# Rope and transpose of each batch's ten tiles moved to slots of their own in a fused attention and mixture kernel

## The reference

```
q = rms_norm(layernorm(x)) * q_norm_w       # 16 heads of 32
k = rms_norm(ctx) * k_norm_w ; v = ctx      # 4 key/value heads, 4 query heads on each
q, k = q*cos + rotate_half(q)*sin, the same for k          # rope
x = x + softmax(causal(q k^T / sqrt(32))) v @ w_out.T
xt = layernorm(x)
probs = softmax(xt @ w_router); top 4 of 128, normalised
basis_k = silu(xt @ w_gate_k) * (xt @ w_up_k)               # k = 0..7, 256 wide
mixed = sum over the top 4 and k of mix * basis_k ; x = x + mixed @ w_down + shared(xt)
```

## Time and profile before

| | |
|---|---|
| runs | 840.81, 843.52, 844.84 us; median 843.52 us |
| the profiled execution | 844.43 us, its span 842.7 us |
| PE | busy 780.9 us (93%) |
| DVE | busy 656.7 us (78%) |
| ACT | busy 578.7 us (69%) |
| POOL | busy 523.7 us (62%) |
| mean granted TensorE clock | 0.974 |
| transfers | 127.02 MB, mean 151 GB/s |

### The profile page before, as it was taken

The page is one execution under the profiler, slowest core; times in us unless marked ns, Lnnn a source line. Parts: engine busy times, 40 slices in busy tenths (PEclk is TensorE's granted clock), DMA queues, the critical chain, the costliest instruction groups (busy, mean ns, idle before and its releaser), DMA issues. The chain is left out here.

```text
span 842.7 us, 15205 instructions
## 1 busy us (share of the span) xinstructions
PE 780.9 (93%) x4180; PEld 617.7 (73%) x4180; DVE 656.7 (78%) x1635; ACT 578.7 (69%) x1413; POOL 523.7 (62%) x685
## 2 busy tenths in 40 slices
PE   2768899899999999989999999989999999999998
PEld 2645567677777778667778788768777887788876
DVE  7657798679888778778888888767878786688774
ACT  3867887577777667677688676658776775654542
POOL 4546457895488556896378745896566624661561
PEclk9967799999999999999999999989999999999999
DMA  8322135445445545643454445435444535454550
GB/s 289 110 67 80 31 131 169 137 142 176 152 157 169 155 154 201 197 142 126 148 204 167 138 136 181 161 126 169 149 165 142 176 116 163 164 187 128 207 190 26
DMA packets 57051, 127.02 MB, mean 151 GB/s; under 512 B 10920, under 2 KB 28040, under 8 KB 56968
## 3 DMA queue, kind: packets, MB, share of 16 engines
q1 hardware_dynamic: 56968, 126.04, 45.1%
HBM read 107.55 MB, written 4.46 MB: 133 GB/s over the span
## 5 line engine op out<-in xcount | busy, mean ns | idle before, releaser
L1606 PE MATMUL u<-w_h,t_h 128*128 128x512 f32 x640 | 259.6, 406 | 9.4 <-POOL w_l L888 7.1
L1606 PE MATMUL u<-w_l,t_h 128*128 128x512 f32 x640 | 251.7, 393 | 0.0
L1606 PE MATMUL u<-w_h,t_l 128*128 128x512 f32 x640 | 251.6, 393 | 0.0
L1259 DVE TENSOR_TENSOR w_l<-w_raw,w_h 128x512 fp32r<-128x512 f32 x288 | 244.8, 877 | 0.0
L930 ACT ACTIVATE w_h<-w_raw 128x512 fp32r<-128x512 f32 x384 | 218.9, 620 | 11.3 <-DMA w_raw<-in_w_units 10.5
L888 POOL TENSOR_TENSOR w_l<-w_raw,w_h 128x512 fp32r<-128x512 f32 x96 | 138.2, 1439 | 102.1 <-ACT w_h L930 101.7
L964 ACT ACTIVATE scores<-scores,mx 128x384 f32<-128x384 f32 (+1 forms) x224 | 128.3, 573 | 76.9 <-DVE mx L1202 75.4
L1202 DVE CUSTOM_DVE_ANT_0 scores<-s,mask_qk 128x384 f32<-128x384 f32 (+1 forms) x224 | 112.3, 503 | 49.0 <-PE s L1482 48.3
L1606 PEld LDWEIGHTS u<-w_h,t_h 128*128 128x128 f32 x640 | 121.4, 190 | 37.9 <-POOL w_l L888 9.9
L896 POOL TENSOR_TENSOR macc<-macc,gb 128x256 f32<-128x256 f32 x112 | 105.0, 939 | 64.6 <-DVE gb L1362 64.4
L1606 PEld LDWEIGHTS u<-w_h,t_l 128*128 128x128 f32 x640 | 120.9, 189 | 27.2
(11 more groups left out here) (150 smaller groups left out, 1208.1 us busy)
## 6 DMA issues: line engine op xcount, KB each, us to landing
w_raw<-in_w_units SPq DMA_DIRECT2D x160, 512.0 KB, 4.2
w_raw<-in_w_out_t SPq DMA_DIRECT2D x16, 512.0 KB, 4.9
w_raw<-in_shared_w_down SPq DMA_DIRECT2D x16, 512.0 KB, 4.5
q_st<-turned_h SPq DMA_DIRECT2D x232, 32.0 KB, 1.9
out<-x SPq DMA_DIRECT2D x16, 256.0 KB, 2.2
q_st<-turned_l SPq DMA_DIRECT2D x116, 32.0 KB, 1.9
x<-in_x SPq DMA_DIRECT2D x3, 1024.0 KB, 9.5
k_st<-turned_h SPq DMA_DIRECT2D x48, 32.0 KB, 2.3
```

Source lines behind the costliest of these rows:

```text
L1259: e.tensor_tensor(w_l[:, i % WR, k, :], w_raw[:, i % WR, k, :], f32(w_h[:, i % WR, k, :]), ALU.subtract).then_inc(s_wl, 1)
L1606: last = e.matmul(u_bank[n % 2][:], t[:, k, cols], ww[:, i % WR, k, :], start=(k == 0 and m == 0), stop=(k == KC - 1 and m == 2))
```

## The change

All ten tiles of a batch get slots of their own, written as offsets from the batch's first slot, one table for batch 1 and one for batches 2 and 3. In absolute slots, from before to after:

| tile of batch 1 | rope | turn |
|---|---|---|
| 10 (keys) | 31 → 33 | 34 → 36 |
| 11 | 37 → 36 | 40 |
| 12 | 43 → 39 | 46 → 43 |
| 13 | 49 → 42 | 52 → 46 |
| 14 | 53 → 45 | 56 → 50 |
| 15 (keys) | 54 → 48 | 57 → 56 |
| 16 | 57 → 51 | 60 |
| 17 | 61 → 59 | 64 |
| 18 | 65 → 64 | 68 → 69 |
| 19 | 73 → 69 | 76 → 74 |

In batch 2 (batch 3 is 48 slots later, but for its last tile, 170 → 165 and 173 → 171): tile 20 79 → 74, 82 → 79; 21 stays at 81 and 84; 22 89 → 85, 92 → 89; 23 97 → 88, 100 → 92; 24 101 → 92, 104 → 97; 25 102 → 95, 105 → 104; 26 105 → 99, 108; 27 109 → 107, 112; 28 113 → 112, 116 → 117; 29 121 → 117, 124 → 123. In batch 0 only the rope of tile 9 moves, 30 → 27. The key squares and scales, query scale and moments of the second halves come 2 to 10 slots earlier, the keys' stacking 2 slots later (first halves) or 1 earlier (second halves). The stacking of queries keeps its slot, except that it follows a later turn (tiles 18, 28, 38: one slot later). No instruction is added or removed.

```diff
-FIRST_TILES = dict(rope=(-34, -32, -20, -12, -7, 6, 9, 16, 23, 30), turn=(-17, -13, -8, -1, 6, 12, 15, 21, 27, 34), stack=(7, 16, 22, 28, 35))
+FIRST_TILES = dict(rope=(-34, -32, -20, -12, -7, 6, 9, 16, 23, 27), turn=(-17, -13, -8, -1, 6, 12, 15, 21, 27, 34), stack=(7, 16, 22, 28, 35))
+SECOND_TILES = dict(rope=(-19, -16, -13, -10, -7, -4, -1, 7, 12, 17), turn=(-16, -12, -9, -6, -2, 4, 8, 12, 17, 22))
+LATER_TILES = dict(rope=(-26, -19, -15, -12, -8, -5, -1, 7, 12, 17), turn=(-21, -16, -11, -8, -3, 4, 8, 12, 17, 23))
...
-QUERY = dict(rope=-3, turn=0, stack=1)
-KEYS = dict(rope=(-21, 2), turn=(-18, 5))
-
-PREP = dict(key_squares=(-39, 4, -29, -8), key_scale=(-36, 5, -26, -1), query_scale=(-35, 9, -23, 4), key_stack=(1, 13, -16, 8))
+
+PREP = dict(key_squares=(-39, 4, -29, -10), key_scale=(-36, 5, -26, -7), query_scale=(-35, 9, -23, -6), key_stack=(1, 13, -14, 7))
...
-MOMENTS = (-39, -38, 4, 7, -32, -27, -6, -1)
+MOMENTS = (-39, -38, 4, 7, -32, -27, -13, -9)
...
-            hb, i = n // NB, n % NB
-            if hb < H:
-                return FIRST_TILES[name][n]
-            if i == 0:
-                return batch_slot(hb // H) + KEYS[name][hb % H]
-            return span_slot(hb * KV + i - 3) + QUERY[name]
+            b, i = n // (H * NB), n % (H * NB)
+            return batch_slot(b) + (FIRST_TILES, SECOND_TILES, LATER_TILES)[min(b, 2)][name][i]
...
-                if s == (FIRST_TILES["stack"][u - U0] if u < H * KV else span_slot(u - 2) + QUERY["stack"]):
+                if s == (FIRST_TILES["stack"][u - U0] if u < H * KV
+                         else max(span_slot(u - 2), tile_slot(query_tile(u), "turn")) + 1):
```

## The result

The changed kernel takes 852.42 us (median of 4 runs, 850.83 to 854.38) against 843.55 us for the kernel before beside it: ratio 1.0111, 95% interval 1.0078 to 1.0144. It is 1.1% slower, where 831.5 us, 1.4% faster, was forecast, and it lies above the range given (826 to 841). The profiled execution took 852.83 us with a span of 851.1 us; before, the span was 842.7 us.

What follows compares the result with a forecast made beforehand. TensorE, busy 780.9 of 842.7 us, was taken as the bound, with GpSimd late at batch borders; 15.2 - 1.5 - 1.0 = 12.7 us off 844.43 gave 831.7, stated as 831.5 us, range 826 to 841.

Steps and rivals of the forecast that it cites:

- SyncE's order: First halves' keys stacked behind maxima and queries instead of before; TensorE waits for none of them, so no cost.
- The ring of turned buffers: `turned_high` must wait for the stacking of the tile two before; cost nothing, up to 1 us at the high end.
- VectorE's added work: Batch 1: two moments and a low part earlier, at slots 39 and 43; with tile 10's later turn, 0 to 3, taken 1.0 us.
- the banks: Moving TensorE's transposes among the three rotating banks, bounded by 0.5 us either way.
- The ports' rule: VectorE and GpSimd lock each other out for whole instructions; ropes against eight `w_l` would cost 6 us, not 0.7.
- Borders, 15.2 gross: TensorE's waits at three batch borders go, 10.4 us, and the clock falls behind them, 4.8 us.
- the floor: The chain projection, VectorE's residual and moments, `norm_scale`, `w_l` keeps 0 to 1.1 us at three borders; taken 0.5 each.
- Tiles 21 and 31, 1.40 us, stay: TensorE's waits of 1.40 us before these tiles remain, as their slots are unchanged.
- The rival "slower, 851 us": New GpSimd backlog in batch 1's slots 42 to 53, 6.3 us a place, three places deciding; chance 0.08.
- the time until slot 44 longer by over 2 us: Sign of being wrong: the start, 110.05 us until slot 44 before, lengthens by over 2 us.
- a batch of 48 slots: Sign of being right: 48 slots take about 190 us in place of 194.
- `turned_high` waiting for transfers: Sign of being wrong: `turned_high` waits for stacking transfers.

Runs made afterwards that it cites:

- the earlier load: Kernel with early keys and VectorE's work back, plus SyncE's shared w_down load started one slot earlier: 831.6 us, ratio 0.9866.
- the three mends: Changed kernel with first halves' keys stacked early again, second halves' key squares two slots later, shared w_down load one slot earlier: 830.54 us, ratio 0.9859.

## Why the prediction was wrong, by its own steps

**SyncE's order, priced at nothing: the step that failed.** The prediction saw that the keys of a first half are stacked behind the queries and said that TensorE waits for none of these transfers. True, and beside the point: what stands behind them in the queue is a weight load for which ScalarE waits, with VectorE's `d_l` and TensorE behind it. So the time that SyncE's issues take, which the sum had at nothing, is what was mis-priced. Twelve issues of 0.63 us make it start 6.7 us later. Measured: 13.5 us in two places, 14 us by the experiment that moves the keys back (852.42 to 838.47), and 13.3 us by the one that moves them late in the kernel before. Of the 7.1 us of slots 88 to 90, 3.84 are the wait and 10 x (1 - 0.72) = 2.8 the clock of that window; of the 6.5 us of slots 136 to 138, 4.31 and 10 x (1 - 0.83) = 1.7.

**The ring of turned buffers, "cost nothing, up to 1 us".** Right for the tiles that it is about: after 44 us no `turned_h` waits for a transfer in the changed kernel. The prediction worked it out for tiles 33 and 35, slot 152; the tighter place is tile 22, whose turn comes three slots after the keys of tile 20 are stacked. There the slack is some 4 us by the estimate above, and the 4.97 us wait needs the load in front of the keys.

**VectorE's added work and the banks, 0 to 3 us, taken 1.0, and 0.5 us either way for the banks.** Measured: 4.9 us at slot 46 in the profile, 3.2 to 3.7 us in time, from the squares of a key tile, which the prediction did not name (it priced moments and a low part, which proved free). 1.75 us of it are the wait; the rest goes, by the inference above, with the clock behind it, which the prediction had at 1.00 from slot 46 on. The bank order makes it a wait of 2.50 us, and half a microsecond was no bound for that: what a bank costs is the lateness of its reader. The ports' rule, set at 6 us for the ropes against the adds, did not come in that size: all 288 `w_l` of VectorE are busy for 248.1 us, where it was 244.8. But in one place a pair took 2.35 us in place of 1.28, and that was where TensorE waited.

**Borders, 15.2 gross, 1.5 for the floor.** Right. 4.8 + 4.0 + 6.2 = 15.0 us came back, where 13.7 were forecast. The three waits for `w_l` left 0.70, 0.74 and 0.69 us, within the 0 to 1.1 given, and the clock in both windows is 1.00. The stretches behind the borders took 1.3 to 2.0 us each, together 4.7, a term that the sum lacked: that is SyncE's queue too, as the earlier load shows.

**Tiles 21 and 31, 1.40 us, stay.** Right: 1.40 and 1.33 us.

**The sum.** Without the late keys and the squares the changed kernel takes 835.1 us, 7.8 below the kernel before beside it, where 12.0 were forecast; with the load early too it takes 830.5. That this is near 831.5 is in part luck: the earlier load is no part of the change, and it also takes from a wait that the kernel before had (0.73 us for `d_l` at 200.36 us). The gain of the borders was there; what was missed is what the move displaced. The rival "slower, 851 us" had the size, but not the place: GpSimd's slots 42 to 53 had no backlog that cost TensorE, and SyncE, the engine without arithmetic, was on no rival's list. Of the signs named beforehand, "the time until slot 44 longer by over 2 us" was there (+4.0), and a batch of 48 slots took 198.7 and 199.1 us where some 190 was the sign of being right; with the three mends it is 190.2 and 191.5. "`turned_high` waiting for transfers" came only where the kernel before has it too (1.45 us at 43.84 us, 1.04 us before).

## What to carry to other kernels

An issue queue is an engine. When a step that issues transfers moves in it, count its issues times their length, and ask for each transfer behind it who waits for that one, not only who waits for those that moved. An experiment that moves a transfer to the front also moves its own wait there, and all that stands behind it waits along; so undo the root (here `key_stack`) as well as the symptom (the load) before calling the cause found, and read in the trace what the experiment's kernel waits for. And a mean over all instructions of a group does not price a meeting of two: look at the rows where both engines run.

## What was not expected of the hardware

- Each stacking transfer of 32 KB holds SyncE's queue for about 0.63 us (twelve in 7.6 us), against 1.05 us for the two of 512 KB of a weight chunk: the issue, not the bytes, sets it.
- The granted clock does not follow the wait alone. Behind a wait of 2.50 us, 110 to 120 us ran at 0.76 in the changed kernel, at 0.68 in the one with early keys, and at 1.00 in the one with only the moments back. The waits of 3.84 to 4.39 us in slots 89 and 90, 137 and 138 were followed by falls in all four kernels that have them.
- Two kernels with the same instructions up to slot 32, the one with the squares back and the one with the moments back, reached it 3.5 us apart in their profiles (-1.3 and +2.2 us against the kernel before). A difference of that size in the start of one profile says nothing.
